# Cross attention in layer 2: scores on four 32-row tiles, maxima kept while copying, subtraction on GpSimd, exponential behind the turn

## The reference, cut to the part that is touched

```python
q = _qdq(x) @ _qdq(wq).T + bq
kv = cond @ wkv.T + bkv
k, v = jnp.split(kv, 2, axis=-1)          # all three to (B, rows, 16 heads, 16)
attn = jax.nn.softmax(jnp.einsum('bnhd,bmhd->bhnm', q, k) * scale, axis=-1)   # scale = 1/4
o = jnp.einsum('bhnm,bmhd->bnhd', attn, v).reshape(B, N, C)
out = _qdq(o) @ _qdq(wp).T + bp           # added to x
```

## Time and profile before

| | us |
|---|---|
| median of 3 runs (2001.55 to 2006.57) | 2006.19 |
| the profiled execution | 1996.45 |
| its span, first to last instruction | 1994.7 |
| the stage that is touched, first to last of its instructions | about 1346 to 1505 |

### The profile page before, as it was taken

How to read it: one execution, slowest core, us unless ns; L and a number is a source line. 1 busy time by engine, 2 the same in 40 slices (tenths; PEclk the granted TensorE clock), 3 DMA queues, 4 the chain that set the end, 5 groups by cost and what they waited for, 6 DMA issues and landing times. The chain is left out here.

```text
span 1994.7 us, 42500 instructions
## 1 busy us (share of the span) xinstructions
PE 1789.1 (90%) x12207; PEld 1210.3 (61%) x12216; DVE 1261.6 (63%) x4137; ACT 1028.1 (52%) x2698; POOL 729.2 (37%) x707
## 2 busy tenths in 40 slices
PE   7999999998999899859899999988997788999765
PEld 4677777776565557635566666654554455887533
DVE  5666666665777635566533433456987954777697
ACT  5555555554333355311344444436888943666586
POOL 3333333332000111557355555653320011998420
PEclk9999999999999999969999999999998899999888
DMA  9990000000000000244577777650001021222100
GB/s 313 305 278 0 0 0 0 0 0 0 0 0 0 1 1 13 72 162 157 129 163 165 170 170 172 111 114 1 1 2 66 1 70 41 48 51 58 35 22 22
DMA packets 145607, 145.55 MB, mean 73 GB/s; under 512 B 49376, under 2 KB 133568, under 8 KB 145344
## 3 DMA queue, kind: packets, MB, share of 16 engines
q1 hardware_dynamic: 122432, 113.81, 19.4%
q0 software_dynamic: 23040, 30.01, 8.4%
HBM read 137.12 MB, written 66.44 MB: 102 GB/s over the span
## 5 line engine op out<-in xcount | busy, mean ns | idle before, releaser
L1711 POOL DMA_INDIRECT expert_sums<-moe_rows_in,moe_to x128 | 198.3, 1550 | 154.0 <-DMA expert_sums<-moe_rows_in,moe_to 76.5
L1977 DVE COPY moe_ht_e<-moe_turned 128x256 f32<-128x256 f32 x128 | 54.3, 424 | 204.4 <-PE moe_turned L1792 201.7
L1784 PE MATMUL moe_gate<-moe_places,moe_xt 128*128 x512 | 175.2, 465 | 3.3 <-issue 1.9
L570 ACT ACTIVATE ga_prob<-ga_score,ga_neg_max 128x128 f32<-128x128 f32 x256 | 99.6, 390 | 125.7 <-DVE ga_neg_max L443 125.7
L2067 POOL TENSOR_TENSOR ln_rstd<-ln_var,half 128x4 f32<-128x4 f32 (+1 forms) x16 | 21.6, 1349 | 365.7 <-DVE ln_var L2063 365.7
L190 POOL TENSOR_TENSOR ga_q_inv<-ga_q_sum,half 128x4 f32<-128x4 f32 x64 | 64.5, 1008 | 224.1 <-DVE ga_q_sum L426 224.1
L3327 DVE CUSTOM_DVE_ANT_0 ctxt<-wa_score,early 128x128 f32<-128x128 f32 x512 | 110.8, 287 | 47.0 <-PE wa_score L3173 46.8
L3143 POOL TENSOR_TENSOR ctxt<-ctxt,wa_top 128x512 f32<-128x512 f32 x128 | 129.9, 1042 | 17.0 <-DVE wa_top L3327 17.0
L325 PE MATMUL ga_summed<-ga_wo,ga_out_t 128*128 128x256 f32 x512 | 121.2, 380 | 0.7 <-ACT ga_out_t L578 0.7
L1784 PEld LDWEIGHTS moe_gate<-moe_places,moe_xt 128*128 128x128 f32 x512 | 90.5, 189 | 48.3 <-issue 13.2
L249 PE MATMUL ga_proj<-early,ga_xt 128*128 128x512 f32 x252 | 118.6, 593 | 0.0
(11 more groups left out here) (491 smaller groups left out, 4700.9 us busy)
## 6 DMA issues: line engine op xcount, KB each, us to landing
moe_places<-in_L_ffn_packed SPq DMA_DIRECT2D x128, 608.0 KB
slot_x<-zeros SPq DMA_DIRECT2D x24, 1076.0 KB, 13.8
moe_rows_in<-slot_x SPq DMA_DIRECT2D x128, 134.5 KB, 2.7
wa_v<-v_ctx SPq DMA_DIRECT2D x16, 180.0 KB, 3.1
early<-in_L_xattn_Wq SPq DMA_DIRECT2D x5, 512.0 KB, 7.8
x<-in_x SPq DMA_DIRECT2D x4, 512.0 KB, 9.9
ga_wo<-in_L_xattn_Wo SPq DMA_DIRECT2D x1, 2048.0 KB, 15.5
expert_sums<-zeros SPq DMA_DIRECT2D x2, 1024.0 KB, 7.8
```

The lines of the kernel that those rows point to most:

```text
L570: last = act.activation(prob[:, n % 2, part], score[:, n % 2, part], ACT.Exp, bias=neg_max[:, n % 2, h:h + 1], accum_out=total[:, n % 2, h ...
L1711: pool.indirect_dma_start(out=mem.sums[j % SUMS], out_offset=bass.IndirectOffsetOnAxis(ap=to[:, j:j + 1], axis=0), in_=y[:, j, :], in_offs ...
L1784: last = pe.matmul(both[j % 2][:, 0:2 * FE], xt[:, j % 2, c, :], packed[:, place, c * 2 * FE:(c + 1) * 2 * FE].rearrange("p a n -> p (a n) ...
```

## The change

- **Scores:** one call `scores(t)` a tile: eight matmuls on 32 rows and 256 columns. The four 32-row parts of the array (`STRIP`) stand side by side, each with two heads' rows (`PAIR`), and each writes its own bank. `kd` needs two copies of the keys in place of four, and GpSimd makes it with one instruction a tile (`spread_keys`), two tiles ahead.
- **Maxima:** for each head VectorE runs one instruction that adds a tile of zeros to the scores, writes the sum to `low` in SBUF and keeps the running maximum in `top`. The score bank is free when it has been read; `below`, `probs` and `bias` are gone.
- **Subtraction:** GpSimd subtracts `top` from `low` in place, one instruction a unit (`lower`).
- **Exponential:** PE turns `low`, and ACT takes the exponential while it copies out of the turned bank. The separate copy is gone.
- **Mixes:** `mix_up(t)` does the 16 heads in one stretch, one tile later.
- `low`, `top` and `pt` have two buffers by tile. VectorE does the scores of tile t+1 during tile t; `count` stands ahead of `round_mixed`.

```diff
-                def scores(t, c):
-                    pe.wait_ge(spread.sem, spread.at(HC * t + c))
...
-                    for half in range(2):
-                        k = 2 * c + half
-                        rows = slice(half * SPLIT, (half + 1) * SPLIT)
...
-                        pe.matmul(score[k][:, :], qt[rows, c, t * P:(t + 1) * P], kd[rows, t % 2, c, :, :],
-                                  start=True, stop=True).then_inc(scored.sem, 1)
+                def scores(t):
+                    pe.wait_ge(spread.sem, spread.at(t))
...
+                    if t >= 1:
+                        pe.wait_ge(topped.sem, topped.at((t - 1) * U + U - 1))
+                    for c in range(HC):
+                        for k in range(U):
+                            rows = slice(k * STRIP, (k + 1) * STRIP)
+                            last = pe.matmul(score[k][:, c * PAIR * P:(c + 1) * PAIR * P], qt[rows, c, t * P:(t + 1) * P], kd[rows, t % 2, c, :, :],
+                                             start=True, stop=True)
...
                 for t in range(B):
                     turn_probs(t, 0)
+                    turn_probs(t, 1)
+                    if t < LASTB:
+                        scores(t + 1)
                     if t >= 1:
-                        mix_up(t - 1, U - 1)
-                    turn_probs(t, 1)
+                        mix_up(t - 1)
                     if t >= 2:
                         turn_mixed(t - 2)
-                    if t < LASTB:
-                        scores(t + 1, 0)
-                    mix_up(t, 0)
+                    turn_probs(t, 2)
                     if t >= 2:
                         go_down(t - 2)
-                    turn_probs(t, 2)
-                    mix_up(t, 1)
                     turn_probs(t, 3)
                     if t >= 1:
                         turn_back(t - 1)
...
                 def exp(t, k):
...
+                    act.activation(pt[:, t % 2, k, :, :].rearrange("p h n -> p (h n)"), turned[k % 2][:, :], ACT.Exp, scale=D ** -0.5).then_inc(pt_moved.sem, 1)
...
+                    for h in range(UH):
+                        ins = dve.tensor_tensor_reduce(low[:, t % 2, k, h, :], score[k][:, h * P:(h + 1) * P], zero[:, :], 1.0, LOWEST,
+                                                       ALU.add, ALU.max, top[:, t % 2, k, h:h + 1])
...
+                def lower(t, k):
+                    pool.wait_ge(topped.sem, topped.at(t * U + k))
+                    unit = low[:, t % 2, k, :, :]
+                    pool.tensor_tensor(unit, unit, top[:, t % 2, k, :].unsqueeze(2).to_broadcast([P, UH, P]), ALU.subtract).then_inc(lowered.sem, 1)
```

More of the change, by code:

```diff
@@ L888 @@
 EARLY = VALUES + 5120
-BY_BIAS = (0, 1)
 class Arena:
@@ L2182, in cross_attention @@
         qt = sb("qt", [P, HC, T])
[L2183 to L2186, removed]
+        own8, own4, own = sb("own8", [P, 2 * UH]), sb("own4", [P, UH]), sb("own", [P, PAIR])
+        zero = sb("zero", [P, P])
+        kd = sb("kd", [P, 2, HC, PAIR, P])
+        top = sb("top", [P, 2, U, UH])
+        low, pt = sb("low", [P, 2, U, UH, P]), sb("pt", [P, 2, U, UH, P])
         mt = sb("mt", [P, U * P])
@@ L2224, in _ @@
                 pool.wait_ge(ready.sem, 3)
-                pool.tensor_tensor(own[:, :], own8[:, 0:UH], own8[:, UH:2 * UH], ALU.add).then_inc(ready.sem, 1)
+                pool.tensor_tensor(own4[:, :], own8[:, 0:UH], own8[:, UH:2 * UH], ALU.add).then_inc(ready.sem, 1)
                 pool.wait_ge(ready.sem, 4)
-                for t in range(B):
[L2228 to L2233, removed]
+                pool.tensor_tensor(own[:, :], own4[:, 0:PAIR], own4[:, PAIR:2 * PAIR], ALU.add).then_inc(ready.sem, 1)
@@ new lines, in bias @@
+                def bias(t):
+                    pool.wait_ge(norm.normed.sem, norm.normed.at(t))
+                    pool.tensor_tensor(mem.x[:, t, :], mem.x[:, t, :], w.bp[:, :], ALU.add).then_inc(biased.sem, 1)
+                spread_keys(0)
+                spread_keys(1)
+                for k in range(U):
+                    lower(0, k)
+                for t in range(B):
+                    for k in range(U):
+                        if t < LASTB:
+                            lower(t + 1, k)
+                        if k == 1 and t + 2 < B:
+                            spread_keys(t + 2)
+                    bias(t)
@@ L2500, in _ @@
                     norm.round(dve, g)
-                lower(0, 0)
-                lower(0, 1)
+                dve.wait_ge(zero_set.sem, 1)
+                for k in range(U):
+                    lower(0, k)
                 for t in range(B):
-                    lower(t, 2)
-                    lower(t, 3)
+                    if t < LASTB:
+                        for k in range(U - 1):
+                            lower(t + 1, k)
                     if t >= 2:
```

105 lines of the change are left out of this document (41 added, 64 removed).

## The result

The changed kernel takes **1986.67 us** (median of 5 runs, 1977.2 to 1989.45), the kernel before 2006.19 (5 runs, 2001.49 to 2014.1): a ratio of 0.990, 95% interval 0.988 to 0.992. The forecast was 1990.2 us in a range of 1982 to 1999; the time lies 3.5 us under the forecast.

What follows compares the result with a forecast made beforehand. TensorE's list was taken to bound the kernel at 7.50 us a tile; the loop through `od` would give 6.65. The stage's 17.0 us less, minus 1.0 for the clock, took 2006.2 to 1990.2 us, range 1982 to 1999.

Steps and rivals of the forecast that it cites:

- the allowance for the clock: Thin head: 1.0 us of the 17.0 gain taken off for TensorE's lower clock, bounds 0 and 2.
- the loop through `od`: Steady loop: waits through the one bank `od`, from addition to next addition, set the new period, 6.65 us a tile.
- rival 2: Loop shorter: ScalarE copies may begin before the one ahead drained, leaving VectorE's 6.32; 4 us more gain, 1986; chance 0.11.
- VectorE second, 0.33 behind: Steady loop: VectorE's list is the largest of any engine, 6.32 us a tile, under the loop's 6.65.
- the rounding chain: VectorE's rounding steps in each tile, taken at 2.11 us of its 6.32 list.
- GpSimd's hold: VectorE's last rounding step may wait for a GpSimd instruction: nothing to 0.84 us a tile, 0.4 covered before the addition.
- Rival 1: Rounding waits a whole GpSimd instruction every time, making VectorE the bound at 7.03 a tile; 4.6 us back, 1995; chance 0.16.
- Head: Stage start: shorter scores and earlier turns let tile 1's scores begin at 1372.9 instead of 1378.21.
- Tail: Stage end: tile 13 is added at 1474.1, before at 1491.14, with the same work behind it; 17.0 us less.
- rival 3: Loop: TensorE falls to 1.2 GHz, its loop steps take twice as long; 52 us, 2042; chance 0.07 with similar slower causes.
- Rivals 4: Score stretch: 32-row matmuls run one after another, some 3.5 us for 1.10; 29 us back, 2019; chance 0.04.

Runs made afterwards that it cites:

- the bias in the head: Changed kernel with the projection's bias for 12 of 16 tiles added by GpSimd ahead of the loop: 1990.85 us, single run.
- the row's turn first: Changed kernel with the rounded row turned ahead of the mixes, projected right behind them and copied ahead of the mixes: 1980.24 us median.
- the row's turn first and the mixes in halves: Kernel with the row's turn first, plus half of a tile's mixes placed ahead of that turn and half behind: 1977.72 us, single run.
- the rounding on ScalarE: Kernel with the row's turn first and the bias in the head, plus VectorE's last rounding step done by ScalarE: 1978.47 us, single run.
- the row's turn first and the bias in the head: Kernel with the row's turn first, plus the bias of 12 tiles added ahead of the loop: 1980.45 us, single run.

## Why the prediction was right

Its size came from the right mechanism, and the terms that were off nearly cancel. Point by point, on the stage (forecast -17.0 before the allowance for the clock, measured -17.8):

- **No engine's list holds the 7.50, the loop through `od` sets the new period:** right, shown by the scores and the turns issued twice and by the bias in the head. Forecast 6.65, the bare loop 6.54, the changed kernel 6.575. In the tile shown in the profile after, from scores to scores, with the forecast in brackets: scores 1.08 (1.10), mixes until ScalarE's copy 1.15 (1.17), that copy 0.49 (0.60), the row's copy until the projection 0.52 (0.52), projection until the addition 1.31 (1.24), addition until the turn back 0.59 (0.54), turn back 0.38 (0.47), the two turns 1.08 (1.01): 6.60 (6.65). The two terms that were too long are durations taken for distances: the mix copy is 0.60 long, but the row's copy starts 0.49 after it (1416.94 and 1417.43), as rival 2 said a copy may. Of the 1.31, 0.07 is VectorE coming late after its long rounding step. Over 12 tiles the period brought 0.9 us more than forecast.
- **TensorE's list sets the pace before:** no run tests this, and the run with the turns twice shows that 30.00 of 30 us busy do not prove it. The rows speak for it: before, the turn back started 0.52 us after the addition had ended (1409.57 to 1410.09), so that handover was not tight; now it is 0.11. The new period does not hang on this.
- **VectorE second, 0.33 behind:** second, but further behind. Its list without holds is 6.08, not 6.32, so the gap to the bare loop is 0.46. The 2.11 of the rounding chain held 0.14 of a hold that tile already had (its last step was 0.49 long), and the statistics' 0.43 is a duration; the next instruction starts 0.34 after them.
- **GpSimd's hold:** the size per meeting lay within the bounds (0.05 to 0.53, bound 0.84), and it was right that the cover before the addition takes most of it: 0.035 a tile is left. Rival 1, that the holds make VectorE the bound in all tiles, does not hold; in every other tile VectorE comes 0.07 late. The Trainium skill (SBUF — State Buffer, section Who interferes with whom) says that a blocked side waits for the whole instruction of the other. The rows agree in so far as the step ended 0.14 to 0.15 us after GpSimd's instruction in all the cases shown here; what is paid is what is left of that instruction, between 0.05 and 0.53.
- **Head:** tile 1's scores came 1.2 us later than forecast (27.99 us after the stage's first turn, forecast 26.84). The forecast had an allowance of 1.0 for the clock, for the thin rounds after tile 0; those ran at 1.00. The loss is ahead of them, in projections that the change doesn't touch. Before and after, busy time and clock of the second 4 us of the stage:

```profile
1350.00:1354.00 4.00, 4.00 (x8) 1.58 (x6) 4.00 (x6) 2.17 (x5) 4.00 (x6) 0.69 0.01 2
```

```profile
1360.00:1364.00 4.00, 4.00 (x6) 1.69 (x5) 3.93 (x9) 2.54 (x5) 1.41 (x2) 0.50 0.01 2
```

TensorE left 1.2 GHz (0.50) later in this execution, though in the 4 us ahead of these it had been busy for as long at 0.50 in both: 2.78 us before, 2.75 after. A projection's weight load took 0.34 us at that level and 0.19 at the upper one; it fell to 0.19 at 6.5 us after the stage's first turn before, and after it was 0.34 up to 8.4 us. With the same code on TensorE up to there, it fell at 8.1 us in the run with the row's turn first and at 6.5 in the one with the row's turn first and the mixes in halves. So this differs from one execution to the next.
- **Tail:** tile 13's addition came as worked out (128.6 us after the stage's first turn, forecast 128.0), but "the work behind it is the same" was off by 1.3 us: before, TensorE ran part of it at the lower level, after not. The granted clock was 0.91 from 1495 to 1496 and 0.50 from 1496 to 1499, behind pauses of TensorE of 1.36 us (until 1494.92) and 0.56 (until 1495.92). Before, from 1495 to 1500 (columns as above):

```profile
1495.00:1500.00 5.00, 4.43 (x20) 3.47 (x21) 4.20 (x14) 1.07 (x2) 0.00 (x0) 0.66 0.00 0
```

In two of the experiments it fell there as well: 0.75 from 1480 to 1485 with the rounding on ScalarE, and 0.73 from 1475 to 1480 with the row's turn first and the bias in the head, where it takes 27.0 us from tile 15's scores to the stage's end, against 25.7 with the row's turn first alone, where it stayed at 1.00. So a fall of the clock, as in rival 3, is real in the thin ends, at about 1.3 us a time. In the loop, where rival 3 put it, it never showed (1.00 from 1400 to 1475).
- **Rivals 4 and 2:** the 32-row matmuls run side by side (1.08 us, forecast 1.10). Rival 2's reason was true by 0.1 us and its end, VectorE's list, was not reached.

The sum of the stage, in us over the forecast: head +1.15, first rounds +0.24, period -0.93, the last two additions +0.06, the end -1.27: -0.75, which leads from -17.0 to the -17.8 measured. The medians differ by 19.5; the 1.7 us beyond the stage lie within what the other stages vary by (10.0 us between the two profiled executions). So that the time came within 3.5 us of the forecast is in part luck; the stage's length is what tests the mechanism.

## What to carry to other kernels

When no engine's list explains the period, follow the one buffer that several steps share around its loop, and price a step by the distance between starts, not by its duration. Here work added inside such a loop cost its full length (0.83 us) and work beside it next to nothing (0.01), though TensorE was then busy all the time; issuing one step twice, once in the loop and once beside it, told which is which. And after a loop is cut, the second bound is near (here VectorE's list, 6.08 us and its holds, under a loop of 6.54), so shortening that engine's list is worth trying only with what it does to the loop priced as well. A pause that a profile does not list can still be one: distances from start to start showed 0.10 us where it listed none.

## What the hardware showed that I had not expected

- Of VectorE's steps in the loop only the last rounding step changed its length beside GpSimd (0.50 to 0.89 in the changed kernel's loop). The 16 instructions a tile that copy and keep the maximum started 0.21 us apart all through the loop, whatever GpSimd did beside them.
- One move, the exponential ahead of the turn or behind it, is worth 0.04 us a tile in the loop and 3.8 us once in the head. Behind the turn the table load (1.28 us from 1384.02) lies beside tile 1's scores (from 1384.08); ahead of it they wait for it.
- Two orders of the same instructions differ by 0.33 us a tile (6.575 and 6.24) with no engine doing less.
